# A transformer block with conditioning and an adapter on one core: 512-column up products, a fourth bank for attention scores, and a relu moved into the normalisation

## The reference

```
# layer 0: attention and SwiGLU
h = gamma * rmsnorm(x) + beta
q, k, v = heads(h @ W_q.T), heads(h @ W_k.T), heads(h @ W_v.T)      # 16 heads of 16
attn = softmax(sqrt(16 / 256) * einsum('bnqd,bnkd->bnqk', q, k))
x = x + a_alpha * (attn @ v) @ W_o.T
x = x + f_alpha * (silu(h @ gate_w.T) * (h @ hidden_w.T) @ out_w.T + out_b)   # h normalised again, 1024 hidden
# layer 1: gated MLP, quantised
h = x * scale * rsqrt(mean(x * x) + eps)
val, gate = split(h @ up_w.T)                                       # 2 x 1024
h = val * gelu(gate)
x = x + act_quant(h) @ weight_quant(down_w).T                       # int8 steps, ternary weights
# layer 2: adapter with weights made per batch
x = x + relu(x @ Wd_b.T + bd) @ Wu_b.T + bu                         # bottleneck 128
# layer 3: layer norm
x = (layernorm(x) * weight + bias + tanh(lin(cond))) * weight + bias
```

## Time and profile before

| | us |
|---|---|
| median of 3 runs | 1068.99 |
| lowest, highest | 1067.8, 1069.29 |
| the profiled execution | 1068.02 |
| its span, first to last instruction | 1066.2 |

### The profile page before, as it was taken

How to read it: one execution, slowest core, us unless ns; L and a number is a source line. 1 busy time by engine, 2 the same in 40 slices (tenths; PEclk the granted TensorE clock), 3 DMA queues, 4 the chain that set the end, 5 groups by cost and what they waited for, 6 DMA issues and landing times.

```text
span 1066.2 us, 22449 instructions
## 1 busy us (share of the span) xinstructions
PE 993.7 (93%) x7442; PEld 848.0 (80%) x7442; DVE 750.6 (70%) x1720; ACT 553.9 (52%) x1166; POOL 192.7 (18%) x246
## 2 busy tenths in 40 slices
PE   5586989999999999999999999999999999998995
PEld 4244759798898979798988979797988979796984
DVE  3725468676777778686777878686767778785645
ACT  3163364655555464656555463646555564645532
POOL 1411421112020201111120201021120202021220
PEclk9576989999999999999999999999999999999997
DMA  8994543040402113040403112030404022130000
GB/s 287 287 343 129 208 149 91 2 140 2 132 8 90 49 45 94 1 139 1 139 1 110 29 62 77 23 116 1 139 1 129 11 80 60 40 90 2 21 21 10
DMA packets 78321, 89.45 MB, mean 84 GB/s; under 512 B 18688, under 2 KB 64912, under 8 KB 75664
## 3 DMA queue, kind: packets, MB, share of 16 engines
q1 hardware_dynamic: 72640, 63.86, 20.1%
q0 software_dynamic: 2304, 16.78, 4.3%
q10 hardware_dynamic: 3344, 8.39, 2.2%
HBM read 63.14 MB, written 25.31 MB: 83 GB/s over the span
## 4 chain that ended last, share of the span: by engine, by line
PE 74%; issue 9%; DVE 6%; ACT 4%; DMA 3%; POOL 1%; SPq 1%; ACTq 0%; DVEq 0%; POOLq 0%
PE bank L695 15%; PE bank L650 15%; PE bank L664 7%; PE bank L619 6%; PE bank L609 5%; PE bank L593 5%; PE bank L567 4%; PE bank L553 3%; PE bank L713 2%; PE bank L576 2%; ACT probs L1005 2%; PE bank L756 2%; PE bank L636 1%; PE bank L727 1%; PE bank L674 1%
## 5 line engine op out<-in xcount | busy, mean ns | idle before, releaser
L1005 ACT ACTIVATE probs<-bank 128x512 f32<-128x512 f32 x256 | 139.6, 598 | 54.9 <-PE bank L609 54.1
L1306 DVE TENSOR_REDUCE neg_max<-bank 128x2 f32<-128x512 f32 x256 | 161.8, 680 | 0.5 <-PE bank L593 0.5
L495 POOL TENSOR_TENSOR act_lo<-act_f,act_hi 128x256 fp32r<-128x256 f32 x120 | 89.7, 753 | 393.4 <-ACT act_hi L1048 393.4
L1042 ACT ACTIVATE silu_g<-bank 128x256 f32<-128x256 f32 x128 | 49.2, 385 | 192.6 <-PE bank L650 192.4
L1084 ACT ACTIVATE gelu_g<-bank,r 128x256 f32<-128x256 f32 x128 | 60.8, 475 | 95.6 <-PE bank L695 94.8
L609 PE MATMUL bank<-q_stack,k_stack 128*128 128x256 f32 x512 | 99.0, 317 | 11.9 <-ACT probs L1005 11.0
L695 PE MATMUL bank<-up_hi,h_hi 128*128 128x256 f32 x512 | 108.7, 294 | 0.9 <-DVE y L1279 0.3
L650 PE MATMUL bank<-h_hi,gh_hi 128*128 128x256 f32 x512 | 103.7, 284 | 4.6 <-DVE h_lo L1367 4.6
L650 PE MATMUL bank<-h_lo,gh_hi 128*128 128x256 f32 x512 | 103.3, 283 | 0.0
L695 PE MATMUL bank<-up_lo,h_hi 128*128 128x256 f32 x512 | 103.1, 283 | 0.0
L650 PE MATMUL bank<-h_hi,gh_lo 128*128 128x256 f32 x512 | 102.9, 283 | 0.0
(11 more groups left out here) (190 smaller groups left out, 2138.6 us busy)
## 6 DMA issues: line engine op xcount, KB each, us to landing
hyper<-w_hyper POOLq DMA_DIRECT2D x16, 1024.0 KB, 6.5
q_stack<-q_dram SPq DMA_DIRECT2D x96, 128.0 KB
k_stack<-k_dram SPq DMA_DIRECT2D x96, 128.0 KB
q_dram<-probs SPq DMA_DIRECT2D x16, 512.0 KB, 2.8
k_dram<-probs SPq DMA_DIRECT2D x16, 512.0 KB, 3.6
x_res<-xT SPq DMA_DIRECT2D x16, 256.0 KB, 2.8
x_in<-xT SPq DMA_DIRECT2D x15, 256.0 KB, 2.7
out<-xc SPq DMA_DIRECT2D x15, 256.0 KB, 2.5
```

The source lines that it names most:

```text
L495: pool.tensor_tensor(act_lo[:, c % 3, :], act_f[:, c % 2, :], act_hi[:, c % 3, :].bitcast(F32), ALU.subtract).then_inc(g_lo.sem, 1)
L1005: act.activation(probs[:, h % SLOTS], halves(SCORE_BANKS[h % 3]), ACT.Exp, scale=float(H / D) ** 0.5).then_inc(s_exp.sem, 1)
L1306: dve.tensor_reduce(neg_max[:, qt, :, pair:pair + 1].rearrange("p a o -> p (a o)"), halves(n % 3), AX_X, ALU.max, negate=True).then_inc(ma ...
```

## The change

It has three parts. The up products put value and gate into one matmul of 512 columns: the moving operand is a view of two blocks of 256 columns, 1024 columns apart, the output is the whole bank; 48 matmuls per batch take the place of 96. The scores get a fourth bank, 4, from head 6 on: heads 7 and later wait for the exp four heads back, and head 6, the first in bank 4, for DVE's step L1288 of `norm_a(nxt)`. The turns change with it: turn 0 has heads 5, 6 and 7 ahead of product 0 and heads 8 to 11 behind it, turn 1 heads 12 to 15 behind product 1, turns 2 and 3 no scores. On DVE the relu of the adapter goes from ahead of `normalise(a, 0)` to a place within it, behind the shuffle; bodies without a batch `a` keep it where it was.

```diff
-SCORE_BANKS = (0, 1, 5)
+SCORE_BANKS = (0, 1, 5, 0, 1, 5, 4, 0, 1, 5, 4, 0, 1, 5, 4, 0)
...
-                def scores(b, h):
+                def scores(b, h, nxt=None):
...
-                    if h >= 3:
-                        pe.wait_ge(s_exp.sem, s_exp.at(b, h - 2))
+                    if h >= 3 and h != 6:
+                        pe.wait_ge(s_exp.sem, s_exp.at(b, h - (2 if h < 6 else 3)))
+                    if h == 6 and nxt:
+                        pe.wait_ge(n1_dve.sem, n1_dve.at(nxt, 4))
                     for k in range(TT):
-                        mm = pe.matmul(halves(SCORE_BANKS[h % 3])[:, k, :], k_stack[:, h, k * P:(k + 1) * P], q_stack[:, h // 2, :],
+                        mm = pe.matmul(halves(SCORE_BANKS[h])[:, k, :], k_stack[:, h, k * P:(k + 1) * P], q_stack[:, h // 2, :],
...
-                    at = halves(7 - n % 2)
-                    for x in range(2):
-                        i = 0
-                        for w, h in ((up_hi, h3_hi), (up_lo, h3_hi), (up_hi, h3_lo)):
-                            for d in range(DC):
-                                mm = pe.matmul(at[:, x, :], h[:, d, t * P:(t + 1) * P],
-                                               w[:, d, x * F + c * UW:x * F + (c + 1) * UW], start=(i == 0), stop=(i == 5))
-                                i += 1
+                    i = 0
+                    for w, h in ((up_hi, h3_hi), (up_lo, h3_hi), (up_hi, h3_lo)):
+                        for d in range(DC):
+                            both = w[:, d, :].rearrange("p (x f) -> p x f", x=2)[:, :, c * UW:(c + 1) * UW]
+                            mm = pe.matmul(halves(7 - n % 2), h[:, d, t * P:(t + 1) * P], both, start=(i == 0), stop=(i == 5))
+                            i += 1
...
-                            if t < 3:
-                                scores(a, 4 * t + 5)
-                                scores(a, 4 * t + 6)
-                            elif nxt:
+                            if t == 0:
+                                for h in range(5, 8):
+                                    scores(a, h, nxt)
+                            elif t == 3 and nxt:
                                 project_v(nxt, 0)
                             attend(a, t)
...
-                        if a:
-                            for h in range(4 * t + 7, min(4 * t + 9, H)):
+                        if a and t < 2:
+                            for h in range(4 * t + 8, 4 * t + 12):
                                 scores(a, h)
...
-                    act.activation(probs[:, h % SLOTS], halves(SCORE_BANKS[h % 3]), ACT.Exp, scale=float(H / D) ** 0.5).then_inc(s_exp.sem, 1)
+                    act.activation(probs[:, h % SLOTS], halves(SCORE_BANKS[h]), ACT.Exp, scale=float(H / D) ** 0.5).then_inc(s_exp.sem, 1)
...
-                def normalise(b, u):
+                def normalise(b, u, between=None):
...
                     dve.stream_shuffle(den[:], den_raw[:], [(DH + i) % 32 for i in range(32)]).then_inc(o_dve.sem, 1)
+                    if between:
+                        relu(between)
                     dve.tensor_scalar(num, tile[:, 0, :], even, None, ALU.mult).then_inc(o_dve.sem, 1)
...
-                    if g:
+                    if g and not a:
                         relu(g)
...
                     if a:
-                        normalise(a, 0)
+                        normalise(a, 0, g)
```

## The result

The changed kernel takes 1050.79 us (median of 4 runs, 1048.74 to 1051.91), the kernel before 1068.65 beside it (4 runs, 1067.8 to 1069.29): a ratio of 0.9825 with an interval of 0.9806 to 0.9843. Forecast were 1049.7 and a range of 1045.5 to 1055. The profiled execution is the lowest of the four, 1048.74 with a span of 1046.9, so the pair of profiles differs by 19.3 us and the medians by 17.9.

A forecast was written before the change was run, and what follows sets the result against it. PE was taken as the bound, with two attention waits costing 1.12 us per body. Savings of 16.9 (waits) and 2.4 (up products) sum to 19.3: 1066.2 - 19.3 = 1046.9, plus 2.8 gives 1049.7 us, range 1045.5 to 1055.

The follow-up runs named there:

- e8: Changed kernel with DVE's scaling of h2 split: multiplication stays after the first act_u, the two scalings come after the second; 1047.26 us, ratio 0.9801.
- e6: Kernel before with only the relu moved inside the normalisation, nothing else; 1068.6 us, ratio 1.0007.

## What to carry to other kernels

When a stall ends, look for the next reader on each chain, not only at the engine that was idle: a second late link (here product 1 behind exp 7) hides in the shadow of the first, and several edits that are worth nothing alone can be worth something together. Lateness of a helper engine costs only what is left after the slack at its next reader, so follow it to a start on the bounding engine before pricing it. An idle time of the weight loads is not one of PE: look at which of the two a wait belongs to before counting it. A cheaper instruction on the bounding engine pays in full only while the engine that frees its banks keeps ahead (product 7 here); a few instructions moved on that other engine (e8) gave three times what the wider matmuls did.

## What the runs showed of the hardware

**A wait costs more than its idle time.** In the changed kernel a wide matmul that starts just after a wait for DVE is followed by the next 0.295 us later instead of 0.23, also where PE itself shows no idle time (products 2 and 7; only their weight loads do); after a longer wait (product 3: 569.46) the first pair takes 0.57 instead of 0.46 (569.46 to 570.03, 570.96 to 571.42).

**The same idle time, another clock.** Ahead of batch 15's output projection PE idles 2.67 us in both kernels. PE of before, then of the changed kernel:

```profile
985.12 1.99 PE L627 MATMUL bank<-o_norm,w_o 128*128 128x256 f32 x8 [2.67 <-DVE o_norm L1341]
```
```profile
966.64 2.96 PE L629 MATMUL bank<-o_norm,w_o 128*128 128x256 f32 x8 [2.67 <-DVE o_norm L1343]
```

Windows over these matmuls and the next, before and after (last columns: granted clock, DMA share, GB/s):

```profile
985.10:987.80 2.70, 2.67 (x12) 2.39 (x13) 1.60 (x4) 1.17 (x3) 0.00 (x0) 1.00 0.00 0
```
```profile
966.60:971.00 4.40, 4.36 (x12) 3.53 (x13) 1.61 (x4) 1.46 (x3) 0.00 (x0) 0.61 0.00 0
```

The same twelve matmuls took 1.7 us more in the changed kernel, at 0.61 of full speed on the mean, that is for most of them at the lower level of 1.2 GHz. What the engine did before was alike in both, and the granted clock had been 1.00 over the 10 us before them. The traces of the twelve experiments have the same 2.67 us of idle time at this place, and in each the twelve matmuls took 4.1 to 5.3 us, also in e6, where they start at 985.64, half a microsecond later than in before. So the trace of before is the exception, by 1.4 us or more, and the two traces of the changed kernel differ by 0.9 here (4.4 and 5.3). What decides it, the moment at which the idle time falls or something else, these traces do not settle; in the comparison of the two profiles it hides 1.7 us of gain.
